# The order in which the two halves of a tile's sums are fetched back from DRAM in a Mamba-2 and MLP layer

## The reference, cut to what matters

```python
z, xBC, dt = jnp.split(u @ W_in, ...)           # d_inner 512, d_state 128, 8 heads of 64
xBC = silu(conv(xBC))                           # 4 taps along the sequence
x, B, C = jnp.split(xBC, ...)
dt = softplus(dt + dt_bias); A = -exp(A_log)
y = ssd(x * dt, A * dt, B, C) + x * D           # y_l = sum over s <= l of (C_l . B_s) exp(sum of A*dt over s+1..l) x_s dt_s
y = y * silu(z)
y = y * rsqrt(mean(y * y) + eps) * norm_scale
h = layernorm(u + y @ W_out)
out = layernorm(h + (gelu(h @ Wg.T) * (h @ Wu.T)) @ Wd.T)
```

## Time and profile before

| | us |
|---|---|
| median of 3 runs | 926.2 (924.76 to 927.67) |
| the profiled execution, its own time | 930.15 |
| its span, from first to last instruction | 928.4 |
| PE busy | 858.1 (92% of the span) |
| DVE busy | 698.9 (75%) |
| ACT busy | 554.3 (60%) |
| share of the chain that ended last put down to the transfers into `dec` | 7% |

### The profile page before, as it was taken

One profiled execution on the slowest core, in us unless ns is written; L12 is line 12 of the kernel. 1 busy time (PEld: TensorE's weight loads), 2 busy tenths in 40 slices (PEclk: granted clock), 3 DMA queues, 4 the chain that ended last, 5 costly groups with the idle time before them and its releaser, 6 DMA issues.

```text
span 928.4 us, 16398 instructions
## 1 busy us (share of the span) xinstructions
PE 858.1 (92%) x5512; PEld 742.8 (80%) x5512; DVE 698.9 (75%) x1588; ACT 554.3 (60%) x1014; POOL 71.4 (8%) x105
## 2 busy tenths in 40 slices
PE   4669798899999999999999999999999999999997
PEld 3448677787898888887888789888888788888886
DVE  6776878787879688886878787877879687857453
ACT  4844687458735776548735775559636774566232
POOL 2110000200020000200020000200020000100000
PEclk9897989899999999999999999999999999999999
DMA  4421440015101420023001420133001410130010
GB/s 144 132 76 39 128 124 24 12 58 161 35 24 68 121 85 23 25 75 139 34 23 68 126 79 23 45 90 128 11 23 69 150 57 12 58 104 1 1 35 12
DMA packets 37578, 61.32 MB, mean 66 GB/s; under 512 B 3264, under 2 KB 25888, under 8 KB 37536
## 3 DMA queue, kind: packets, MB, share of 16 engines
q1 hardware_dynamic: 37104, 60.76, 20.5%
q10 hardware_dynamic: 432, 0.03, 0.0%
HBM read 51.94 MB, written 4.64 MB: 61 GB/s over the span
## 4 chain that ended last, share of the span: by engine, by line
PE 65%; DVE 10%; DMA 9%; issue 7%; ACT 5%; POOL 3%; SPq 1%; DVEq 0%; POOLq 0%; ACTq 0%
DMA dec<-spread 7%; PE gate_bank L540 5%; PE up_bank L540 5%; PE up_bank L542 5%; PE up_bank L541 5%; PE gate_bank L542 5%; PE gate_bank L541 5%; PE mixer L540 5%; PE down L540 4%; PE down L541 4%; PE down L542 4%; PE mixer L541 4%; PE mixer L542 4%; PE mixer L607 3%; ACT dec L770 2%
## 5 line engine op out<-in xcount | busy, mean ns | idle before, releaser
L540 PE MATMUL down<-wd_hi,in_hi 128*128 128x256 f32 x512 | 144.1, 282 | 0.7 <-DVE in_lo L1068 0.7
L541 PE MATMUL down<-wd_lo,in_hi 128*128 128x256 f32 x512 | 142.9, 279 | 0.0
L542 PE MATMUL down<-wd_hi,in_lo 128*128 128x256 f32 x512 | 142.6, 278 | 0.0
L937 DVE SCALAR_TENSOR_TENSOR xbc<-mixer,chan,xbc 128x510 f32<-128x510 f32 (+1 forms) x162 | 111.1, 686 | 25.2 <-ACT xbc L738 24.3
L540 PE MATMUL gate_bank<-hT_hi,wg_hi 128*128 128x512 f32 (+1 forms) x288 | 113.2, 393 | 11.4 <-ACT act_sb L803 11.4
L789 ACT ACTIVATE in_hi<-act_sb 128x512 fp32r<-128x512 f32 (+1 forms) x144 | 83.0, 576 | 64.1 <-PE down L542 53.0
L1082 DVE SCALAR_TENSOR_TENSOR act_sb<-up_bank,act_sb 128x512 f32<-128x512 f32 (+1 forms) x144 | 90.6, 629 | 39.9 <-PE up_bank L542 20.0
L1068 DVE TENSOR_TENSOR in_lo<-act_sb,in_hi 128x512 fp32r<-128x512 f32 (+1 forms) x144 | 90.2, 627 | 40.2 <-ACT in_hi L789 39.7
L540 PE MATMUL up_bank<-hT_hi,wu_hi 128*128 128x512 f32 (+1 forms) x288 | 107.0, 371 | 5.6 <-DVE act_sb L1082 5.6
L803 ACT ACTIVATE act_sb<-gate_bank 128x512 f32<-128x512 f32 (+1 forms) x144 | 79.0, 549 | 50.4 <-PE gate_bank L542 49.8
L542 PE MATMUL up_bank<-hT_hi,wu_lo 128*128 128x512 f32 (+1 forms) x288 | 107.0, 371 | 0.0
(11 more groups left out here) (183 smaller groups left out, 1868.5 us busy)
## 6 DMA issues: line engine op xcount, KB each, us to landing
low<-spread SPq DMA_DIRECT2D x32, 512.0 KB, 3.8
dec<-spread SPq DMA_DIRECT2D x32, 512.0 KB, 6.1
state_decay<-spread SPq DMA_DIRECT2D x32, 128.0 KB, 7.4
xbc<-in_u_t_dram SPq DMA_DIRECT2D x7, 512.0 KB, 3.7
h_sb<-in_u_dram SPq DMA_DIRECT2D x7, 512.0 KB, 3.8
h_res<-h_sb SPq DMA_DIRECT2D x7, 512.0 KB, 2.9
out_dram<-h_res SPq DMA_DIRECT2D x7, 512.0 KB, 2.9
scales<-in_ffn_s_dram SPq DMA_DIRECT2D x24, 128.0 KB, 2.2
```

What stands on the lines that cost most here:

```text
L540: nc.tensor.matmul(dst, lh, rh, start=first, stop=False, skip_group_check=True)
L541: nc.tensor.matmul(dst, lh, rl, start=False, stop=False, skip_group_check=True)
L542: return nc.tensor.matmul(dst, ll, rh, start=False, stop=last, skip_group_check=True)
L937: ins = stt(acc[:, :, d:], src[:, :, 0:SEQ - d], chan[:, c:c + 1], acc[:, :, d:], ALU.mult, ALU.add)
```

## The change

In `spread_sums` the two loads of a tile change places, each together with the wait that stands before it: first `dec` (upper sums), then `low` (lower sums). Line 465 of before becomes line 459, line 460 becomes line 465. Nothing else changes.

```diff
                 for i in [i for i in which if i < tiles(g)]:
 
                     if i >= 2:
-                        wait_for((exp_in, g, i - 1))
-                    elif kind_of(g) == "first" and i:
-
-                        sp.wait_ge(winz_ok.sem, JT)
-                    sp.dma_start(low[:, i % 2, :, :], of_tile(1, i).partition_broadcast(P)).then_inc(lo_in[i % 2].sem, 16)
-                    if i >= 2:
                         wait_for(ready_at(g, f"Y{i - 2}"))
                     elif kind_of(g) != "first":
                         wait_for(ready_at(g - 1, f"Y{tiles(g - 1) - 2 + i}"))
                     sp.dma_start(dec[:, i % 2, :, :], of_tile(0, i).partition_broadcast(P)).then_inc(hi_in[i % 2].sem, 16)
+                    if i >= 2:
+                        wait_for((exp_in, g, i - 1))
+                    elif kind_of(g) == "first" and i:
+
+                        sp.wait_ge(winz_ok.sem, JT)
+                    sp.dma_start(low[:, i % 2, :, :], of_tile(1, i).partition_broadcast(P)).then_inc(lo_in[i % 2].sem, 16)
```

More of the change, by code:

```diff
@@ L455, in spread_sums @@
                     if i >= 2:
+                        wait_for(ready_at(g, f"Y{i - 2}"))
+                    elif kind_of(g) != "first":
+                        wait_for(ready_at(g - 1, f"Y{tiles(g - 1) - 2 + i}"))
+                    sp.dma_start(dec[:, i % 2, :, :], of_tile(0, i).partition_broadcast(P)).then_inc(hi_in[i % 2].sem, 16)
+                    if i >= 2:
                         wait_for((exp_in, g, i - 1))
```

## The result

| | before | after |
|---|---|---|
| median, us | 928.0 (924.8 to 929.5, 6 runs) | 919.2 (916.7 to 923.4, 6 runs) |
| ratio, with its 95% interval | | 0.9908 (0.9886 to 0.9929) |
| the profiled execution / its span, us | 930.15 / 928.4 | 923.38 / 921.6 |

The forecast was 6.5 us less, 919.7 us from a median of 926.2; with the runs taken beside the changed kernel the median of before has moved to 928.0, so the ratio is the thing to compare: 0.993 forecast, 0.991 measured.

What follows compares the result with a forecast made beforehand. PE, busy 92% of the span, was taken as the bound, so only its idle time counts. Stages 1 to 6 3.8, last stage 2.25, stage 0 0.5, first stage 0: 6.55 us off 926.2 gives 919.7 us, range 917.5 to 923.8.

Steps and rivals of the forecast that it cites:

- Stages 1 to 6: Y's six waits on PE for W, behind ACT's wait for dec, vanish: 3.8 us gained.
- Last stage: H starts some 2.3 us earlier, covering PE's waits of 1.37 and 0.88 us: 2.25 us gained.
- step 3: Last stage: dec in low's place lands at about 826.3, after ACT is free at 825.86; 2.25 us gained.
- Stage 0: Tile 0 gains 0 because PE comes late with its own work; tile 2 gives 0.5 us (between 0 and 1.1).
- rival U: Whole change, put before its rerun: order also does something PE's waits don't show; 8 to 9 us again, ratio 0.991.
- Tile 2's term: Stage 0, tile 2: DVE's stream gains its 0.48 us idle before L, and PE moves by it once: 0.5 us.
- First stage: H's gain ends at DVE's value(6), which waits for the scales: 0 us, at most 0.8.
- A: All stages: order doesn't decide landing, dec still takes 6.2 us; 2.2 us gained, 924.0 us; chance 10%.
- B: Full stages: PE gives the gain back waiting for act_sb; only the last stage's 2.25 us remains, 924.0 us; chance 9%.
- C: Second transfer, low, lands too late for L on DVE; eight stages lose about 1 us each, 934 us; chance 3%.
- D: First stage not held at the scales (0.8) and stage 0 gains 1.1: sum 8.0 us, 918.2 us; chance 13%.

Runs made afterwards that it cites:

- low sixth: Against the kernel before: in each stage both decs, low of tile 1, state_decay, then low of tile 0 behind them all; ratio 0.9984 (0.9966 to 1.0003).

## Why the prediction was right, and where it fell short

**The number.** 919.7 us was forecast and 919.2 measured, and that they lie so near is partly luck: the gain was 2 to 3 us larger than the 6.5 of the sum, and the median of before turned out 1.8 us higher than the 926.2 that it was taken from.

**What bounds the kernel, and the mechanism: right.** The wait that counted was PE's for Y, behind ACT's wait for dec. Dec took low's place and time: 4.0 us where 4.1 was forecast, low 5.9 for 6.2. ACT's wait was to fall under 1.5 us; it fell to 0.3. DVE was never to wait for low but for a tenth; it doesn't wait for it at all.

**Stages 1 to 6: mechanism right, a little under-sized.** All six waits of Y are gone, and no other wait of PE grew in these stages. From the trace of before to that of the changed kernel stages 1 to 5 lose 3.7 us from store to store (515.8 to 512.1 us). The trace of before was one with long waits: in three further traces with the old order for tiles 0 and 1 there (tiles 2 and 3 alone, last stage alone, first stage and stage 0 alone) these five stages take 515.0, 515.1 and 515.6 us, and the waits of Y in them are 2.5, 2.6 and 3.0 us where they were 0.68 + 0.77 + 0.89 + 0.42 + 0.32 = 3.1 us in the trace of before. All traces with dec first for tiles 0 and 1 and low second or third take 512.0 to 512.2 us. So in each of the four a stage loses its wait plus 0.1 us; between the trace of before and that of the changed kernel this rest lies in PE's busy time (504.7 and 504.2 us), and why is open. The timing of the part, 4.4 us (3.2 to 5.7), holds the forecast's 3.8.

**Last stage: right.** 2.25 forecast, 2.4 timed; the profile shows 2.56. H starts at 821.89 after a wait of 0.30 us, dec having landed at 821.8, so the first place's 4 us and not ACT was the limit by then, as step 3 had it. H comes 5.4 us behind the stage's store, where it was 7.9: 2.5 us earlier for the 2.3 forecast.

**Stage 0: the one term that was wrong in its mechanism.** The working said of tile 0: "PE doesn't wait for its W", gain 0, since PE came late with its own work. PE did come late, but because it had waited on the same chain at another place, which that step doesn't name. The copy `wd_lo` (L814), for the unpacking of weights, stands right behind H on ACT. Timelines of ACT and PE before:

```profile
113.27 2.45 ACT L770 ACTIVATE dec<-dec,sum_hi 128x128 f32<-128x128 f32 x8 [2.33 <-DMA dec<-spread]
115.62 0.58 ACT L814 ACTIVATE wd_lo<-down 128x512 fp32r<-128x512 f32 x1
...
116.34 1.19 PE L689 MATMUL down<-h_res,ident 128*128 128x512 f32 x1 [3.97 <-ACT wd_lo L814]
```

and after:

```profile
111.66 2.45 ACT L770 ACTIVATE dec<-dec,sum_hi 128x128 f32<-128x128 f32 x8
114.01 0.57 ACT L814 ACTIVATE wd_lo<-down 128x512 fp32r<-128x512 f32 x1
...
114.73 0.67 PE L689 MATMUL down<-h_res,ident 128*128 128x512 f32 x1 [1.67 <-ACT wd_lo L814]
...
119.24 1.09 PE L607 MATMUL mixer<-dec,xdt 128*64 128x128 f32 x16 [1.08 <-DVE dec L986]
```

The wait of 3.97 us, one of PE's four longest in the whole program, is 2.3 us shorter; PE reaches Y of tile 0 early and waits there for 1.08 us that it didn't wait before. Net 1.2 us of idle time where the sum had 0. (That stage 0 still has two waits near 1.1 us, as was said ahead, is luck: one of them is this new one.)

The idle time is not all. The first matmul in these rows takes 1.19 us before and 0.67 after, for the granted clock of PE fell to half (1.2 of 2.4 GHz) just before the long wait ended. From the stage's store to Y of tile 0, first in the kernel before, then in the one changed in stages 1 to 6 alone (old order here), then in the changed kernel; the fourth row is the stretch at half clock in the kernel before (columns as above):

```profile
104.72:122.53 17.81, 13.50 (x68) 0.81 0.54 166
...
104.40:120.58 16.18, 12.25 (x68) 0.89 0.64 183
...
105.21:119.24 14.03, 10.86 (x68) 1.00 0.72 210
...
115.60:122.40 6.80, 6.06 (x21) 0.50 0.19 43
```

The same 68 instructions keep PE busy for 13.5, 12.3 and 10.9 us. It is so in every trace: the five with the old order for tile 0 of stage 0 wait 3.5 to 4.2 us for wd_lo, have 3.4 or 6.8 us at half clock from there on, and reach Y 16.2 to 18.0 us behind the store. The eight with dec first and low second or third wait 1.5 to 1.7 us, have no such stretch, and reach Y at 13.7 to 14.0. With low sixth the wait for wd_lo is short too, but PE waits 3.3 us for W instead, and 3.4 us at half clock stand behind that wait. So up to Y stage 0 gains 2.2 to 4.2 us, of which the waits explain about 1. This is something that PE's waits don't show, as rival U had put it for the whole change.

Part of it is given back later in the stage. All six traces with dec first in all four tiles of stage 0 have another 3.4 us at half clock, some 43 us behind the store; the two with dec first in tiles 0 and 1 alone have none there. From the store to the end of the wait for h_sb, in the kernel before, in the changed one, and with tiles 0 and 1 alone:

```profile
104.72:172.20 67.48, 54.71 (x416) 0.93 0.30 91
...
105.21:169.97 64.76, 53.50 (x415) 0.97 0.32 95
...
103.79:167.03 63.24, 52.05 (x415) 0.99 0.34 98
```

Over all traces that is 65.2 to 67.5 us with the old order in tile 0, 64.5 to 64.8 with the new one in all tiles, and 63.0 to 63.2 with it in tiles 0 and 1 alone. What brings the later stretch isn't shown. It would fit the lowest median of all, that of dec, dec, low, low with tiles 2 and 3 as before, but tiles 0 and 1 alone timed no better than the whole change.

Tile 2's term, 0.5 us, has no support either: its part alone (tiles 2 and 3) gives nothing that the timing can see, and the wait for act_sb that it rests on, 1.10 us, is 0.54 to 0.72 us in all other traces, of both orders. SP's place in the stage moves too: it gets to the pair of tile 2 some 20 us behind the stage's store, where it was 23.6 (22 to 24 in the five traces with the old order for tile 0).

**First stage: can't be told.** ACT starts H without a wait there, and PE's wait of 5.9 us ahead of XT is 4.9. But DVE's value(6) starts 13.6 us behind the store in both traces, having idled 1.55 us before it where it was 0.62: what H gains does end there, as forecast, and PE then waits 1.42 us before Y. The stretch as a whole takes 77.9 to 79.5 us in the five traces with the old order and 76.4 to 79.3 in the nine with the new one; it differs more between executions of one order than between orders, so that a gain under 1 us can't be told from none.

**What is left.** Stages 1 to 6 were timed at 4.4 us and the last at 2.4, which leaves 1.7 and 2.6 us of the 8.5 and 9.4 us of the whole for the first stage and stage 0. Timed alone they give 1.0 us (-0.1 to 2.2), and by the traces stage 0 is 0.4 to 3.0 us shorter up to h_sb. So the parts and the whole agree within their intervals, and the sum's 0.5 us for stage 0 was most likely the term that fell short. How much of the rest is the clock and how much the chance of the executions stays open: behind h_sb stage 0 has a further stretch at half clock, 3.4 to 13.7 us in either order, that hides a difference of this size.

**The rivals.** A (the order doesn't decide) and B (given back) are refuted by the trace after: dec takes 4 us as first, and PE's waits for act_sb fell from 11.4 to 10.2 us. C didn't come about with low as second, and did with low as sixth. D's number, 918.2 us, or 8.0 us less, is near the measured one, but not for its reasons: the first stage was held at the scales, and stage 0 gained by another way.

## What to carry to other kernels

Two transfers of the same size in one queue land one behind the other, and the order of asking is free: ask first for the one whose reader is itself waited for. Read the gain first from the bounding engine's waits, not from the transfer or its reader (13.1 us of ACT's waits were worth some 8 us), and for every such wait go through all that stands behind the waiting instruction on its engine: the copy behind H held PE for longer than the chain I was following. Give the half that is now second a deadline: if it lands, from the second place, before its reader starts, it costs nothing. And look at the granted clock on both sides of a long wait of PE: here a wait of 4 us was followed by matmuls at half speed, and shortening it gave back more than its idle time, though a part was lost again further on.

## What the runs showed of the hardware

**A place in the queue has no fixed price.** All transfers here are 512 KB, spread from 4 KB over 128 partitions. Landings in stage 2, in us after the issue of the first, issues 0.4 to 0.6 us apart:

| order | first | second | third | fourth |
|---|---|---|---|---|
| low, dec, low, dec (before) | 4.1 | 6.8 | 8.1 | 9.9 |
| dec, low, dec, low (after) | 4.0 | 6.3 | 7.6 | 9.6 |
| low, low, dec, dec | 3.9 | 5.3 | 6.6 | 8.2 |
| dec, dec, low, low | 4.2 | 5.5 | 7.2 | 9.4 |

Over the nine stages of each of these traces the second comes 1.8 to 3.0 us behind the first where the two alternate, and 1.2 to 1.6 where both are of one kind. The same source rows don't bring the alternating order down, nor do neighbouring buffers. What does, both together or something else, wasn't tried. In every trace these 512 KB loads land in the order of their issue. The Trainium skill, SBUF — State Buffer, section "The DMA setup-cost knee", fits one transfer as about 2 us plus bytes over 436 GB/s. The part for the bytes, 1.2 us for 512 KB, taken as an estimate of the step, is near what the second kind of order shows and half of what the alternating one takes.

**Stretches at half clock differ from execution to execution.** The granted clock of PE falls to half (1.2 of 2.4 GHz) mostly in the first stages, where PE idles most (17.6 and 12.8 us in the first stage and stage 0 of the kernel before, 1.9 to 2.5 in stages 1 to 5), and in some executions for longer than in others. The changed kernel's two traces, windows of stage 0, of the half-clock stretch at its end, and of a full stage:

```profile
105.21:207.11 101.90, 90.63 (x582) 0.92 0.24 74
169.04:182.69 13.65, 12.72 (x45) 0.50 0.01 2
412.03:514.51 102.48, 100.90 (x650) 1.00 0.20 67
```

```profile
104.85:202.11 97.26, 86.03 (x582) 0.96 0.25 77
169.10:172.50 3.40, 2.99 (x14) 0.50 0.00 0
409.50:512.00 102.50, 100.92 (x649) 1.00 0.20 67
```

The same kernel takes 101.9 or 97.3 us for stage 0, with 13.7 or 3.4 us at half clock behind the same wait of PE (3.58 and 3.57 us for h_sb). Its stages 1 to 5 agree to 0.05 us each. Stage 6 has such a stretch, of 3.4 us, in some executions of either order, and then takes 1.2 us more (98.5 or 97.3 in the changed kernel). So the traces of this program can be compared stage by stage for stages 1 to 5, which no stretch at half clock touches: to a tenth of a microsecond with the new order, while with the old one a stage differs by up to 0.6 us (102.9 to 103.6 us for stage 3) as H waits longer or shorter. In the first 200 us a change of half a microsecond needs another way to be seen than by the total.
